# A graph-attention and routed-experts kernel: score matmuls stacked per head, and the softmax's inverse sums applied to the attention output

## The reference

```
xn = layernorm(x)
q, k, v = heads(xn @ Wq.T), heads(xn @ Wk.T), heads(xn @ Wv.T)      # 16 heads of 32
a = q k^T * 512**-0.5 + (adj + adj)                                 # per head, 128 x 128
p = softmax(a), a row that is all zero gives p = 0
x = x + (p v) @ Wo.T
# routed experts on all 8192 rows of layernorm(x): gate, top 2 of 8 experts,
# weights max(p, 0.1) / sum, y = x @ expert_W[e] + expert_b[e], summed and halved
x = x + experts(layernorm(x))
```

## Time and profile before

| | |
|---|---|
| median of 3 runs | 1900.24 us |
| the profiled execution, its own time | 1902.03 us |
| its span in the profile | 1900.2 us |
| busy over the span | PE 1714.6, DVE 1347.7, POOL 894.8, ACT 886.5 us |
| phase A: first and last score matmul start | 52.2 and 1340.4 us |
| phase B: from about 1410 us | to the end |
| granted TensorE clock, mean | 0.969 |

### The profile page before, as it was taken

How to read it: one execution, slowest core, us unless ns; L and a number is a source line. 1 busy time by engine, 2 the same in 40 slices (tenths; PEclk the granted TensorE clock), 3 DMA queues, 4 the chain that set the end, 5 groups by cost and what they waited for, 6 DMA issues and landing times. The chain is left out here.

```text
span 1900.2 us, 41822 instructions
## 1 busy us (share of the span) xinstructions
PE 1714.6 (90%) x11600; PEld 1381.2 (73%) x11600; DVE 1347.7 (71%) x4756; ACT 886.5 (47%) x2924; POOL 894.8 (47%) x1468
## 2 busy tenths in 40 slices
PE   4999999999999999999999999999536999999996
PEld 3777777777777777777777777776425778888885
DVE  4668787888888888888888888887543455555554
ACT  2566665656665656566666666665301111111111
POOL 2235444445444444544444544444423456655655
PEclk8999999999999999999999999999758999999998
DMA  6324344334434433433433433433278989888987
GB/s 205 88 66 114 110 115 123 104 104 121 122 101 123 117 99 111 121 115 107 131 104 109 119 118 103 129 93 99 82 266 225 264 177 175 165 164 164 167 158 106
DMA packets 185201, 251.07 MB, mean 132 GB/s; under 512 B 18192, under 2 KB 91920, under 8 KB 184848
## 3 DMA queue, kind: packets, MB, share of 16 engines
q1 hardware_dynamic: 131936, 136.77, 25.7%
q0 software_dynamic: 29680, 69.55, 18.1%
q10 hardware_dynamic: 23360, 42.08, 7.0%
HBM read 105.59 MB, written 109.19 MB: 113 GB/s over the span
## 5 line engine op out<-in xcount | busy, mean ns | idle before, releaser
L561 ACT ACTIVATE prob<-prob,nmax 128x128 f32<-128x128 f32 x1024 | 400.4, 393 | 370.1 <-DVE amax L682 370.1
L942 POOL TENSOR_TENSOR prob<-prob,rinv 128x512 f32<-128x512 f32 x256 | 276.5, 1100 | 237.4 <-DVE rinv L705 236.9
L1142 POOL DMA_INDIRECT out<-yt,token x135 | 212.0, 1571 | 220.1 <-DVE yt L1108 90.5
L678 DVE CUSTOM_DVE_ANT_0 prob<-ps_s,bias 128x128 f32<-128x128 f32 x1024 | 236.5, 286 | 73.0 <-PE ps_s L367 55.5
L1078 ACT ACTIVATE xgT_hi<-ps_x 128x512 fp32r<-128x512 f32 x135 | 80.8, 598 | 415.3 <-PE ps_x L1050 310.0
L1062 PE MATMUL ps_y<-we_hi,xgT_hi 128*128 x540 | 229.0, 424 | 22.0 <-DVE xgT_lo L1097 10.9
L1064 PE MATMUL ps_y<-we_hi,xgT_lo 128*128 x540 | 216.4, 401 | 0.0
L1063 PE MATMUL ps_y<-we_lo,xgT_hi 128*128 x540 | 216.2, 400 | 0.0
L923 POOL TENSOR_SCALAR var<-mv 128x1 f32<-128x1 f32 (+1 forms) x96 | 21.6, 225 | 366.2 <-DVE mv L851 271.4
L561 ACT ACTIVATION_READ_ACCUMULATOR prob<-prob,nmax 128x1 f32 x1024 | 193.5, 189 | 0.0
L616 ACT ACTIVATE pT<-ps_t 128x512 f32<-128x512 f32 x256 | 151.1, 590 | 82.5 <-PE ps_t L436 82.1
(11 more groups left out here) (153 smaller groups left out, 4591.5 us busy)
## 6 DMA issues: line engine op xcount, KB each, us to landing
xg<-x_lists ACTq DMA_DIRECT2D x135, 260.5 KB
kblk<-kT SPq DMA_DIRECT2D x256, 128.0 KB, 2.8
xin<-x SPq DMA_DIRECT2D x64, 256.0 KB, 2.9
xres<-x SPq DMA_DIRECT2D x64, 256.0 KB, 2.6
out<-xres SPq DMA_DIRECT2D x64, 256.0 KB, 2.8
e_stage<-expert_W SPq DMA_DIRECT2D x32, 256.0 KB, 3.9
e_parts<-e_hi SPq DMA_DIRECT2D x32, 256.0 KB, 3.0
e_parts<-e_lo SPq DMA_DIRECT2D x32, 256.0 KB, 3.7
```

Source lines behind the costliest of these rows:

```text
L561: last = nc.scalar.activation(prob[:, r, c, h, :], prob[:, r, c, h, :], ACT.Exp, bias=nmax[:, r, n:n + 1], scale=-1.0, accum_out=rsum[:, r ...
L678: last = nc.vector.tensor_tensor_reduce(out=prob[:, r, c, h, :], in0=ps_s[c % 2][:, P * h:P * h + P], in1=bias[:, b.ring(4), :], scale=-1. ...
L942: tt(prob[:, r, q], prob[:, r, q], rinv[:, r, HC * q:HC * q + HC].unsqueeze(2).to_broadcast([P, HC, P]), ALU.mult)\
L1142: pool.indirect_dma_start(out=out, out_offset=bass.IndirectOffsetOnAxis(ap=token[:, m, :], axis=0), in_=yt[:, r, :], in_offset=None, compu ...
```

## The change

All of phase A is written again: slots are numbered by `t` from -6 to 71 in plain Python, with the same split of a slot in four chunks. What is computed in it differs in these points:

- Scores. SyncE stacks for each graph and each of the four heads of a row group the three parts on 96 partitions: K as (hi, lo, hi) in `ks`, Q as (hi, hi, lo) in `qs`, by 12 DMAs of 32 partitions x 2 KB for K and 12 for Q. Each head's scores are then one f32r matmul of 96 rows and 128 columns, four per chunk. `kblk` and its zeroing are gone. The low parts of K and Q are written in two halves, one for each graph of the pair.
- Softmax. The probabilities are transposed as the exponentials give them. The inverse sums are widened on VectorE to 128x512 (`rwide`, each head's value 32 times), TensorE transposes them (unit R), ScalarE copies them into `oT`, and VectorE multiplies the attention output by them (`weigh_heads`). ScalarE makes the high part from that SBUF tile and GpSimd the low part.
- Both layernorms are applied on ScalarE (`first_norm`, `second_norm`: scale and offset per row); GpSimd's chain makes the offset too, 8 steps for 6.
- Transposes X, X2 and R have a bank of their own (`ps_m`), probabilities one bank (`ps_t`) instead of two, and TensorE's order in a chunk is scores, `times_v`, `transpose_probs`, the small transposes, the projection. O moves from chunk 1 to chunk 2, the residual to chunk 3. The scatter has four semaphores instead of two.

The diff, cut to its core:

```diff
-        QUARTERS = ([[("Q", 0, 1)], [("X2", -3, 0), ("O", -2, 0)], [("K", 2, 0)], [("K", 2, 1)]],
-                    [[("V", 1, 0)], [("X", 3, 0), ("O", -2, 0)], [("X", 3, 1), ("Q", 1, 0)], [("X2", -3, 0), ("V", 1, 1)]])
+        def big(t, c):
+            p = t // 2
+            kind, n, part = ([("K", p + 1, 0), ("K", p + 1, 1), ("O", t - 2, 0), ("Q", p + 1, 0)],
+                             [("Q", p + 1, 1), ("V", p + 1, 0), ("O", t - 2, 0), ("V", p + 1, 1)])[t % 2][c]
+            return (kind, n, part) if (ok(n) if kind == "O" else okp(n)) else None
+        def small(t, c):
+            if t % 2 and c < 2:
+                return ("X", t // 2 + 2, c) if okp(t // 2 + 2) else None
+            if c == 2:
+                return ("X2", t - 3, 0) if ok(t - 3) else None
+            if c == 3:
+                return ("R", t - 1, 0) if ok(t - 1) else None
...
-                        for h in range(HC):
-                            rows = slice(HD * h, HD * h + HD)
-                            sp.dma_start(kblk[rows, r, :, P * h:P * h + P].bitcast(f32),
-                                         kT[rows, :, :, P * r:P * r + P].rearrange("p a c t -> p (a c) t").bitcast(f32)).then_inc(kblk_in[r], 16)
+            def stack(tile, parts, b, done):
+                r = b % 2
+                for i, part in enumerate(parts):
+                    for h in range(HC):
+                        sp.dma_start(tile[HD * i:HD * i + HD, r, h, :, :].rearrange("p c t -> p (c t)").bitcast(f32),
+                                     part[HD * h:HD * h + HD, r, :, :].rearrange("p c t -> p (c t)").bitcast(f32)).then_inc(done[r], 16)
+            def stack_k(b):
+                hold(k_lo_done, 2 * (b // 2) + 2)
+                if b >= 2:
+                    hold(s_full, 4 * (b - 2) + 4)
+                stack(ks, (kT_hi, kT_lo, kT_hi), b, ks_in)
...
-                three(ps_s[c % 2][:, :], qT_hi[:, c, t], qT_lo[:, c, t], kblk[:, r, c, :], kblk[:, r, DC + c, :], True, True).then_inc(s_full, 1)
+                for h in range(HC):
+                    last = mm(ps_s[c % 2][:, P * h:P * h + P], qs[:, r, h, c, :], ks[:, r, h, c, :], start=True, stop=True)
...
-                pe.wait_ge(prob_done, b.count(4, c + 1))
+                pe.wait_ge(exp_done, n + 1)
...
+                        in_ = rwide[:, HC * i:HC * i + HC, :].rearrange("p h d -> p (h d)")
...
+                if kind == "K":
+                    act.wait_ge(K_full, 2 * n + part + 1)
+                    if n >= 1:
+                        for r in range(2):
+                            act.wait_ge(ks_in[r], STACK * n)
...
+            def first_norm(b):
+                k = b % 4
+                act.wait_ge(rstd1_step, RSTD * (b // 2) + RSTD)
+                nc.scalar.activation(xin[:, k, :], xin[:, k, :], ACT.Identity, bias=off1[:, k:k + 1], scale=rstd1[:, k:k + 1]).then_inc(xn_done, 1)
...
+                dve.wait_ge(exp_done, DC * b + DC)
+                nc.vector.reciprocal(rinv[:, r, :], rsum[:, r, :]).then_inc(rinv_step, 1)
...
+                nc.vector.scalar_tensor_tensor(out=rwide[:, :, :], in0=amax[:, r, :].unsqueeze(2).to_broadcast([P, H, HD]), scalar=0.0,
+                                               in1=rinv[:, r, :].unsqueeze(2).to_broadcast([P, H, HD]),
+                                               op0=ALU.not_equal, op1=ALU.mult).then_inc(rinv_step, 1)
+            def weigh_heads(b):
+                dve.wait_ge(rT_done, b + 1)
+                dve.wait_ge(pv_done, DC * b + DC)
+                tt(oT[:, :, :].rearrange("p c t -> p (c t)"), ps_o[:, :], oT[:, :, :].rearrange("p c t -> p (c t)"), ALU.mult).then_inc(oT_done, 1)
...
-                            for q in (2 * c, 2 * c + 1):
-                                tt(prob[:, r, q], prob[:, r, q], rinv[:, r, HC * q:HC * q + HC].unsqueeze(2).to_broadcast([P, HC, P]), ALU.mult)\
-                                    .then_inc(prob_done, 1)
+                        tt(oT_lo[:, :, :], oT[:, :, :], oT_hi[:, :, :].bitcast(f32), ALU.subtract).then_inc(oT_lo_done, 1)
```

More of the change, by code:

```diff
@@ L235, in number @@
[L235 to L249, removed]
@@ L269, in phase_a @@
[L269 to L277, removed]
+        FIRST, LAST = -6, B + 7
+        ok = lambda b: 0 <= b < B
+        okp = lambda p: 0 <= p < B // 2
+        def big(t, c):
[3 more added lines that the diff above has]
+            return (kind, n, part) if (ok(n) if kind == "O" else okp(n)) else None
@@ L367, in three, with wait_bank @@
                 return mm(out_, lhs_lo, rhs_hi, start=False, stop=last)
[L369 to L377, removed]
-                    return
[L379 to L382, removed]
+            def wait_bank(before):
+                if before:
+                    pe.wait_ge(*emptied(before))
@@ new lines, in transposes @@
+            def transposes(t, c):
+                unit = small(t, c)
+                if not unit:
+                    return
+                kind, n, part = unit
+                if kind == "X":
+                    pe.wait_ge(xn_done, 2 * n + 2)
+                elif kind == "R":
+                    pe.wait_ge(rinv_step, 2 * n + 2)
+                else:
+                    pe.wait_ge(xn2_done, n + 1)
+                wait_bank(before_in(small, 1, t, c))
+                for i in range(DC):
+                    if kind == "X":
+                        cc, r = 2 * part + i // 2, i % 2
+                        in_ = xin[:, 2 * (n % 2) + r, P * cc:P * cc + P]
+                    elif kind == "R":
+                        in_ = rwide[:, HC * i:HC * i + HC, :].rearrange("p h d -> p (h d)")
+                    else:
+                        in_ = xn2[:, n % 4, P * i:P * i + P]
+                    last = nc.tensor.transpose(ps_m[:, P * i:P * i + P], in_, ident)
+                last.then_inc({"X": X_full, "X2": X2_full, "R": R_full}[kind], 1)
@@ new lines, in project @@
+            def project(t, c):
+                unit = big(t, c)
+                if not unit:
+                    return
+                kind, n, part = unit
+                bank, r = ps_p[c % 2], n % 2
+                if kind == "O":
+                    pe.wait_ge(oT_lo_done, n + 1)
+                    if n == 0:
+                        pe.wait_ge(w_lo_done, 4)
+                    wait_bank(before_in(big, 2, t, c))
+                    for i in range(DC):
+                        last = three(bank[:, :], oT_hi[:, i, :], oT_lo[:, i, :], w_hi["o"][:, i, :], w_lo["o"][:, i, :], i == 0, i == DC - 1)
+                    last.then_inc(O_full, 1)
+                elif kind == "V":
+                    if n == 0:
+                        pe.wait_ge(w_lo_done, 3)
+                    wait_bank(before_in(big, 2, t, c))
+                    own = slice(P * part, P * part + P)
+                    for i in range(DC):
+                        last = three(bank[:, :], xT_hi[:, r, i, own], xT_lo[:, r, i, own], w_hi["v"][:, i, :], w_lo["v"][:, i, :], i == 0, i == DC - 1)
+                    last.then_inc(V_full, 1)
+                else:
+                    if kind == "K":
+                        pe.wait_ge(xT_lo_done, 2 * n + 2)
+                    if n == 0:
@@ L516, in _, with halves, read_projection @@
             matrix_hi(1, "q")
-            def read(g, j, n):
-                kind, it, part, count = use(g, j, n)
-                if not it.valid or kind == "O":
+            def halves(tile, part, bank):
+                return (tile[:, :, 2 * part:2 * part + 2, :].rearrange("p g c t -> p c g t"),
+                        bank[:, :].rearrange("p (c g t) -> p c g t", c=2, g=2))
+            def read_projection(t, c):
+                unit = big(t, c)
+                if not unit or unit[0] == "O":
@@ new lines, in low_part @@
+                kind, n, part = unit
+                lo, hi, hi_done, done = (kT_lo, kT_hi, k_hi_done, k_lo_done) if kind == "K" else (qT_lo, qT_hi, q_hi_done, q_lo_done)
+                of = ps_p[c % 2][:, :].rearrange("p (c g t) -> p c g t", c=2, g=2)
+                dve.wait_ge(hi_done, 2 * n + part + 1)
+                for g in range(2):
+                    to, less = (w[:, g, 2 * part:2 * part + 2, :] for w in (lo, hi))
+                    if kind == "K":
+                        last = tt(to, of[:, :, g, :], less.bitcast(f32), ALU.subtract)
+                    else:
+                        last = nc.vector.scalar_tensor_tensor(out=to, in0=of[:, :, g, :], scalar=SCALE, in1=less.bitcast(f32),
+                                                              op0=ALU.mult, op1=ALU.subtract)
@@ L985, in phase_b @@
+            for k in range(4):
+                pool.wait_ge(scattered[k], 32 * (B // 4))
 def phase_b(nc, v):
```

819 lines of the change are left out of this document (385 added, 434 removed).

## The result

The changed kernel takes 1931.12 us, median of 4 runs (1929.61 to 1933.48), against 1899.63 us for the kernel before on the same chip: ratio 1.0168, 95% interval 1.015 to 1.0185. It is 1.7% slower where I had forecast 4.5% faster, and outside my range of 1780 to 1905. The profiled execution took 1931.89 us.

The account below looks back on a forecast made before the run. TensorE's own stream bounds phase A, with about 4% lost to VectorE's lateness. 63.75 x (20.21 - 18.85) = 87 us less, +2 at the ends: 1902.0 - 85 = 1817, or 1815 by the median; range 1780 to 1905.

Parts of the forecast that it names:

- TensorE, scores: Phase A score matmuls: four narrow f32r matmuls take 0.54 us a chunk instead of 0.77, saving 1.84 us a pair.
- the rival of the slow narrow matmul: TensorE's scores: 128-column f32r matmuls run slowly, 0.21 to 1.18 us for four or each; priced at 1935 us, chance 0.16.
- TensorE, the rest, and the sum: TensorE in phase A: unit R adds 0.8 us a pair, stream 37.7 a pair; whole time 1815 us.
- VectorE, ScalarE, GpSimd busy: Phase A busy time a pair: VectorE 30.3 us, ScalarE 29.1, GpSimd 15.8, against TensorE's 37.7.
- Walking the even slot ... TensorE hardly waits ... I add nothing: Even slot, `weigh_heads` to O: input ready half a microsecond early; cost 0, range 0 to 1.5 us a pair.
- 0.33 to 0.64, I take 0.45 ... Cost 0: SyncE's stack DMAs: 0.45 us an issue, 27 of 37.7 us a pair; cost 0, bounds 0 to 4.
- Everything but TensorE is late: Phase A: `choose`-to-O chain or SyncE's issues set the pace, TensorE waits 2 to 4 us a pair; chance 0.2.
- its sign: Phase A waits: O for GpSimd's `oT_lo`, or ScalarE's K copy for `ks` stacks, by over 1 us a pair.
- The ends: Start and drain of phase A: first scores 5 us later, drain 3 us shorter, `kblk` zeroing 0; +2 us.
- Phase B stayed, as forecast: Phase B, 1420 to 1900 us: code unchanged, carried over at 480 us, TensorE busy 443.

Follow-up runs that it names:

- the block scores: Changed kernel with the kernel before's block-diagonal K tile and three 512-column score matmuls a chunk, `weigh_heads` first in even slots: 1870.35 us, 0.9876.
- the DRAM version: Changed kernel with all three stack parts filled over DRAM, even graph's Q stack read ahead of the residual load, `weigh_heads` first in even slots: 1821.42 us, 0.9607.
- the table: Four kernels with `weigh_heads` late and early: changed 1931.1, 1940.2; two parts 1915.8, 1829.3; over DRAM 1895.7, 1821.4; block-diagonal 1950.0, 1870.4 us.
- the late place: `weigh_heads` behind chunk 0's minimum in VectorE's even slots, as in the changed kernel: 1931.12 us.
- the early place: Changed kernel with `weigh_heads` moved ahead of chunk 0's minimum in VectorE's even slots, nothing else: 1940.18 us, 1.0217.
- either one alone: Changed kernel with only `weigh_heads` first, 1940.18 us, or only fewer issues: two stacked parts 1915.78, over DRAM with Q read ahead of residual load 1895.7.
- the two together: Changed kernel with `weigh_heads` first and fewer issues: two stacked parts 1829.26 us, or over DRAM with Q read ahead of residual load 1821.42.
- the version with two parts: Changed kernel with two of three stacked parts (16 stack DMAs a graph, Q's low part left out) and `weigh_heads` first in even slots: 1829.26 us, 0.9639.

## Why the prediction was wrong

**TensorE, scores: right.** 0.49 us a chunk, forecast 0.54; the rival of the slow narrow matmul (0.16) is refuted. Nor did the block scores do better: the stacked ones of the DRAM version beat them by 49 us, and by 64 in the stream alone (68.6 to 1265.7 us against 53.3 to 1314.3), near the 59 that 1.84 us a pair come to.

**TensorE, the rest, and the sum: right as the stream's own length.** I had 37.7 us a pair; the DRAM version has a pair of 37.46, and 1821 us against my 1815. What I called the forecast is about what the kernel takes when nobody is late. That the two totals lie so close is in part luck: by the spans of the profiled executions the DRAM version saves 91 us in the stream where I had 87, starts 16 later where I had 5, and ends 9 sooner where I had 3.

**VectorE, ScalarE, GpSimd busy: right in the main.** VectorE 590.9 of 800 us, down from 653; the norms take 0.80 and 0.82 us where I took 0.75; `oT_lo` 1.30, as `e_lo` had said. None is the bound by its sum, and none of these sums tells of the loss.

**"Walking the even slot ... TensorE hardly waits ... I add nothing": the step that failed first.** I followed `oT` forward, to `oT_hi`, `oT_lo` and O in chunk 2, and found it just in time. I didn't follow it to the other reader of the same semaphore: `times_v` of the next graph's chunk 0 writes the one `ps_o` that `weigh_heads` reads, and stands in TensorE's chunk 1 directly behind the scores, ahead of the K projection that could have covered it. In the kernel before `times_v` stood behind the projections. I had named `choose` making VectorE 3 us late; the wait is 2.56 in the pair shown and 1.9 on average. The edit "TensorE's order in a chunk" was listed in the change and had no price in my sum; by the table the late place costs 74 to 87 us where nothing else limits, 2.3 to 2.7 us a pair, against my upper bound of 1.5 (48 us).

**"0.33 to 0.64, I take 0.45 ... Cost 0": the second.** An issue takes 0.59 (median), and the 12 of the K stack 8.5 us with the longer ones and the gaps (802.53 to 811.0), 0.71 each, above my upper end. I reasoned that a small contiguous piece is nearer to the plain load, that is by bytes and shape; `kblk`'s 0.64 was the row of the same kind, SBUF to SBUF over 32 partitions, and should have decided. For the cost I then tried the 0.64 on this one stack alone, and had it start at 14.5 us, as if SyncE were free there: 25.0 us, "still just in time" for ScalarE at about 26. ScalarE did come at about 26 us (808.84). But SyncE was not free: it was still on the Q stacks of the even graph until 799.6, and then stood 1.8 us for the stored residual to land. So the stacks started at 20.1, took 8.5 and 1.4 more to land: 30.0, 3.65 us late. I had the round as a whole at 0.64 in the rival (36 of 37.7 us, "nearly full"; measured 35.6 of issues in the pair), and did not carry it into the cost. By the runs this step is worth 119 us with the other mended, against my upper bound of 4 us a pair (128 us) and the 0 that I took.

**The rival "Everything but TensorE is late" (0.2)** had the causes nearly right: ScalarE's K copy waits for the stacks by 3.8 us a pair, as its sign said, and `weigh_heads` behind `choose` is late, though the waiter is `times_v` and not O. TensorE is idle for 2.9 us a pair. I let it end at 1911, with 3 us more a pair. It left out that TensorE's work itself becomes slower: 39.0 us busy a pair at a clock of 0.96 (745.18 us over the 19.1 pairs that 800 us hold) against 37.4 at 1.00 in the DRAM version. So of the 4.1 us a pair between the two, 2.5 are idle time and 1.6 longer work, which is the 4% that the clock is lower.

**The ends.** First score +10.0 us, forecast +5: the low part of Q was there at 44.8, but SyncE spent 14.5 us on the 12 K stacks of the first graph (1.2 each) and was on two loads until 53.1; the 12 for Q took 7.5 more. Drain -6.8, forecast -3. Phase B stayed, as forecast (busy 447 of 480 us, before 443).

What stays open: why most issues take 0.59 us and some in a burst up to 2.2; and why the early place is 9 us slower than the late one while SyncE is full (the mean granted clock of the whole execution is 0.935, not 0.942). A version with all of it in one set of DMAs, without the trip over DRAM, was not tried, nor was issuing a part of the stacks from another engine, nor moving the residual's load away from its store.

## What to carry to other kernels

When an order is rewritten, list for each semaphore every reader, those that wait to overwrite as well as those that wait to read, and ask what stands between the wait and the nearest long piece of work on the waiting engine. Price the issuing engine's round as a sum like any other engine's: number of DMAs times the issue time of the row most alike in kind, not in bytes, plus what it waits for in its own order; and let each transfer start where that round lets it. And when removing one suspect brings nothing, remove it together with the next before acquitting it: here either one alone changed the time by +9 to -35 us, and the two together by -102 and -110.

## What the runs showed of the hardware

- An issue from SyncE of an SBUF to SBUF copy over 32 partitions took 0.591 us (median) at 64 KB, at 32 KB and at 1 KB. A read of 256 KB from DRAM over as many partitions took 0.43 (302/432/1327 ns), a write of 512 KB 0.38 to 0.46. The Trainium skill ("DMA: Bandwidth & Descriptors", section Issuing engines are not separate DMA queues) says of the time on the sequencer that it is usually small beside the DMA; here it was 0.59 beside 2.0 us to landing, and with 24 a graph the sequencer, not the DMA engines (busy 0.57), was full. The measurement decides.
- DMA engines busy for 0.84 of the time, in the DRAM version, did not slow the pair (37.46 us, and 38.0 on average in the version with two parts, at 0.51), though a residual store then took 5.7 us to land (median) where it had taken 2.2.
- An idle stretch of 2.56 us of TensorE was followed by steps of 0.22 us for 0.12, at a granted clock of 0.70 from 809.98 to 814.00; in the versions without such a stretch the clock was 1.00 from 400 to 1200 us.
